# Two self attentions of a decoder: maxima split without a copy, and their fold and row transfers moved inside the round

## The chip, the cores and the metric

The kernel runs on one core of a Trainium2 chip. Its time is the device time of one execution in microseconds, lower is better. The engines are TensorE (PE, its weight loads PEld), VectorE (DVE), ScalarE (ACT), GpSimd (POOL) and SyncE (SP, which only issues transfers). Each engine runs its own instruction stream in order and waits on semaphores.

## The reference

Two decoder layers on x of 8 x 256 x 256 (8 sequences, 256 positions, width 256). Each layer is a self attention, a cross attention and a mixture of experts, each behind a layer norm and added to x. The change touches the two self attentions (16 heads of width 16, causal; the second has 4 groups of keys and values):

```python
scores = jnp.einsum('bhqd,bhkd->bhqk', q, k) / jnp.sqrt(jnp.float32(hd))
scores = scores + (bias + causal)[None]
attn = jax.nn.softmax(scores, axis=-1)
out = jnp.einsum('bhqk,bhkd->bhqd', attn, v)
```

## The kernel before

Each of the five engines has its program written out by hand; `q.wait_ge(at(name, ...))` waits until the event of that name has happened, and `then_inc(*up(name, ...))` signals it. `Banks.take` gives out the eight PSUM banks in rings and makes a taker wait for the last user of the bank.

A self attention (`Attention`, layer L = 0 or 1) works through the 8 batches in rounds i from -2 to 8. Round i attends with batch i and at the same time computes the scores of batch i + 1 for their maxima only. A round has 12 units u, three for each group g of four heads (kind 0, 1 and 2).

- Scores for the maxima (`pe_scores`, lines 462 and 464): twelve groups for each batch; four before the units, the last one, 11, at unit 9. VectorE takes the maxima (`dve_max`, L608).
- `dve_np` (L614 to L620, unit 10) makes minus the maximum into three bf16 parts in `NP`, so that their sum is exact: the first part, the rest `mr` in fp32, the rest rounded to bf16 by a copy, and what is left.
- `pe_fold` (L473) transposes the parts on TensorE. `act_mT` (L716) copies them to SBUF on ScalarE, and `act_mrow` (L737) issues three transfers from ScalarE's queue that put them as rows 101 to 103 into the queries of batch i + 1. All three stood after the 12 units.
- `pe_attend_s` (L482, in each unit) computes transposed scores minus the maxima of batch i. Its first one in a round waits for the three row transfers (event `mrow`). `act_exp` (L721) is the exponential on ScalarE, `pool_keep` (L787) the causal cut on GpSimd.
- `pe_attend_v` (L495 for kinds 0 and 1, L499 for kind 2) multiplies with the values; group g - 1 in units 5, 8 and 11, so group 2 in unit 11. Group 3 comes in the next round, after the first two score groups and before `pe_v` and two more score groups. `act_out` (L727) copies the outputs; `pe_fin1` (L508) and what follows finish the batch.
- Beside this, `act_hi`, `dve_res`, `act_mid`, `pool_lo` (L793) split the queries and keys of batch i + 3 into parts, and `sp_stack` on SyncE stacks them through DRAM into `q_parts` and `k_parts`. `beside` runs one step of other work (layer 0: products for the cross attention, L228 with ctxT; layer 1: its keys and values, lines 1578 to 1676).

Of the kernel before, what the change touches and what calls it, by code (L numbers as in the profile page):

```python
# [10 lines left out]
ALU = mybir.AluOpType  # L11
# [133 lines left out]
def decoder(nc, I, out):  # L145
    with ExitStack() as ctx:
# [144 lines left out]
        def ln_turn(q, s, p, ring):  # L291
            if s not in (2, 5):
                ln_before[s, p] = ln_before.get("now")
                ln_before["now"] = (s, p)
            b, free = banks.take(ring, ("ln", s, p), [("xnT", s, p)])
            q.wait_ge(at("consts", "all"), *free)
            for j in (0, 1):
                q.wait_ge(at("xn", s, 2 * p + j))
                for k in (0, 1):
                    mm = q.e.transpose(PS[b][:, 256 * k + 128 * j:256 * k + 128 * j + 128],  # L300
                                       normed(s, 2 * p + j)[:, 128 * k:128 * k + 128], idf[:, :])
            mm.then_inc(*up("ln_t", s, p))
# [42 lines left out]
        def steps(g, n=1):  # L345

            while n and g:
                if next(g[0], "end") == "end":
                    g.pop(0)
                n -= 1  # L350
# [8 lines left out]
        class Attention:  # L359
# [163 lines left out]
            def tensor(self, q):  # L523
                L, rp = self.L, self.rp
                kv = [kv_tensor(q, rp) if L == 1 else mix_tensor(q, rp)]
                ln_turn(q, self.ln, 0, rp)
                for i in range(-2, B + 1):
                    n, b, f, p = 0 <= i + 1 < B, 0 <= i < B, i >= 1, self.ahead(i)
                    if i < 0:
                        self.pe_qk(q, i + 2, 0)  # L530
                        self.pe_qk(q, i + 2, 1)
                        if i == -2 or L == 1:
                            ln_turn(q, self.ln, i + 3, rp)
                    if n:
                        self.pe_scores(q, i + 1, 0)
                        self.pe_scores(q, i + 1, 1)
                    if f:
                        self.pe_attend_v(q, i - 1, 3)
                    if n:
                        self.pe_v(q, i + 1, 0)  # L540
                        self.pe_scores(q, i + 1, 2)
                        self.pe_v(q, i + 1, 1)
                        self.pe_scores(q, i + 1, 3)
                    for u in range(12):
                        if b:
                            self.pe_attend_s(q, i, u // 3, u % 3)
                        if n and u in self.FIRST:
                            self.pe_scores(q, i + 1, self.FIRST[u])
                        if u == 0 and self.norms(i - 1):
                            ln_turn(q, *self.norms(i - 1), rp)  # L550
                        if L == 0 and u == 2 and i == -1:
                            ln_turn(q, self.ln, 2, rp)
                        if f and u in (1, 2):
                            self.pe_fin1(q, i - 1, u - 1)
                        if p and u in (3, 6):
                            self.pe_qk(q, p, u // 6)
                        if f and L == 0 and u in (7, 8):
                            self.pe_fin2(q, i - 1, u - 7)
                        if b and u in (5, 8, 11):
                            self.pe_attend_v(q, i, u // 3 - 1)  # L560
                        if f and L == 0 and u in (9, 10):
                            self.pe_fin3(q, i - 1, u - 9)
                        self.beside(u, i, kv)
                    if n:
                        self.pe_fold(q, i + 1)
                steps(kv, 999)


# [41 lines left out]
            def dve_np(self, q, b):  # L610

                L, e, m, mr, NP = self.L, q.e, self.m, self.mr, self.NP
                q.wait_ge(at("mx", L, b, 11), at("fold", L, b - 1))
                e.tensor_scalar(NP[:, :, 0, :], m, -1.0, None, ALU.mult).then_inc(*q.step())  # L614
                q.wait_ge(q.chain())
                e.scalar_tensor_tensor(out=mr, in0=m, scalar=-1.0, in1=NP[:, :, 0, :], op0=ALU.mult, op1=ALU.subtract).then_inc(*q.step())
                q.wait_ge(q.chain())
                e.tensor_copy(NP[:, :, 1, :], mr).then_inc(*q.step())
                q.wait_ge(q.chain())
                e.tensor_tensor(NP[:, :, 2, :], mr, NP[:, :, 1, :], ALU.subtract).then_inc(*up("NP", L, b))  # L620

# [122 lines left out]
            def scalar(self, q):  # L744
                L = self.L
                kv = [kv_scalar(q) if L == 1 else mix_scalar(q)]
                self.act_rows(q, 0)
                ln_copy(q, self.ln, 0)
                for i in range(-2, B + 1):
                    n, b, f, p = 0 <= i + 1 < B, 0 <= i < B, i >= 1, self.ahead(i)  # L750
                    if i < 0:
                        self.act_hi(q, i + 2, 0)
                        self.act_hi(q, i + 2, 1)
                        self.act_mid(q, i + 2, 0)
                        self.act_mid(q, i + 2, 1)
                        if i == -2 or L == 1:
                            ln_copy(q, self.ln, i + 3)
                    if f:
                        self.act_out(q, i - 1, 3)
                    for u in range(12):  # L760
                        if u == 1 and self.norms(i - 1):
                            ln_copy(q, *self.norms(i - 1))
                        if L == 0 and u == 3 and i == -1:
                            ln_copy(q, self.ln, 2)
                        if p and u in (4, 7):
                            self.act_hi(q, p, u // 7)
                        if b:
                            self.act_exp(q, i, u // 3, u % 3)
                        if f and L == 0 and u in (8, 9):
                            self.act_fin2(q, i - 1, u - 8)  # L770
                        if p and u in (6, 9):
                            self.act_mid(q, p, u // 9)
                        if b and u == 9:
                            self.act_out(q, i, 1)
                        self.beside(u, i, kv)
                    if n:
                        self.act_mT(q, i + 1)
                        self.act_mrow(q, i + 1)
                steps(kv, 999)


# [786 lines left out]
        def kv_tensor(q, ring):  # L1568
            for c in range(4):
                bk, free = banks.take(ring, ("kv", c), [("kv_f", c)])  # L1570
                q.wait_ge(at("w_cr1", "bp"), at("w_xa", "r"), *free)
                pair_mms(q, PS[bk][:, :], [(ctxT[:, k, 128 * c:128 * c + 128], wkv[:, k, :]) for k in range(2)]).then_inc(*up("kv", c))
                yield
                yield
                bk, free = banks.take(ring, ("kv_v", c), [("kv_vT", c)])
                q.wait_ge(at("kv_f", c), *free)
                for m in range(2):
                    mm = q.e.transpose(PS[bk][:, 128 * m:128 * m + 128], kv_f[:, 256 + 128 * m:384 + 128 * m], idf[:, :])
                mm.then_inc(*up("kv_v", c))
                for _ in range(12):  # L1580
                    yield
                bk, free = banks.take(ring, ("kv_k", c), [("kv_kM", c, 1)])
                q.wait_ge(at("kv_3", c), *free)
                for g in range(8):
                    mm = q.e.transpose(PB[bk][:, 128 * g:128 * g + 128], K3[:, 2 * g:2 * g + 2, :].rearrange("p h c -> p (h c)"), idb[:, :])
                mm.then_inc(*up("kv_k", c))
                yield
            for _ in range(6):
                yield
            bk, free = banks.take(ring, ("kv_q",), [("kv_Vq",)])  # L1590
            q.wait_ge(at("kv_q8"), *free)
            for c in range(4):

                keys = vq[:, :, 256 * (c // 2):256 * (c // 2) + 256].rearrange("p m (n o) -> p m o n", o=2)
                for m in range(2):
                    mm = q.e.transpose(PB[bk][:, 256 * c + 128 * m:256 * c + 128 * m + 128], keys[:, m, c % 2, :], idb[:, :])
            mm.then_inc(*up("kv_q"))
# [582 lines left out]
```

## Time and profile before

| | |
|---|---|
| median of 3 runs | 1379.77 us (1377.14 to 1382.55) |
| the profiled execution | 1379.55 us, its span 1377.5 us |
| TensorE matmuls busy | 1154.4 us, 84% of the span |
| VectorE busy | 897.2 us, 65% |
| ScalarE busy | 632.4 us, 46% |
| GpSimd busy | 577.2 us, 42% |
| mean granted clock of TensorE | 0.913 |

The layer-0 attention runs from the start to about 220 us, the layer-1 attention from about 590 to 790 us. Busy time counts the instructions of an engine, not the issue of transfers. The granted clock is the share of TensorE's 2.4 GHz that it was given.

### The profile page before, as it was taken

The numbers are of one execution on the slowest core, as the hardware profiler recorded it, in microseconds if no ns is written. First come the engines' busy times: TensorE is split into PE (matmuls) and PEld (weight loads), VectorE is DVE, ScalarE is ACT, GpSimd is POOL, SyncE is SP. The second block draws the span as 40 slices with busy tenths as digits, with TensorE's granted clock in tenths as the row PEclk, the third lists the DMA queues.
The fourth block names the chain that finished last, engine by engine and source line by source line (L and its number), as shares of the span: only waits on it lengthen the run. The fifth ranks groups of instructions, "written<-read, shape, count | busy, mean of one in ns | idle before, by whom it ended". The sixth has DMA issues, their size and how long they took to land.

```text
span 1377.5 us, 24811 instructions
## 1 busy us (share of the span) xinstructions
PE 1154.4 (84%) x7679; PEld 811.0 (59%) x7679; DVE 897.2 (65%) x2501; ACT 632.4 (46%) x1432; POOL 577.2 (42%) x886
## 2 busy tenths in 40 slices
PE   3699989983899999767888587778778778999988
PEld 3577757772466666545666345555556555788855
DVE  4576763665333322277977489999999974656557
ACT  3164653331211111214554389888889861433300
POOL 6143542245511111114655444466655654455510
PEclk8799999996899999969998889988888889999999
DMA  5776644112111111155551110000000004455465
GB/s 135 198 209 158 190 109 160 41 47 93 53 46 47 47 47 47 51 164 152 131 147 42 55 75 1 2 33 33 21 21 25 33 32 142 119 159 158 148 179 144
DMA packets 75805, 127.10 MB, mean 92 GB/s; under 512 B 11703, under 2 KB 59063, under 8 KB 72279
## 3 DMA queue, kind: packets, MB, share of 16 engines
q1 hardware_dynamic: 62142, 95.13, 25.1%
q0 software_dynamic: 10272, 28.39, 5.6%
q10 hardware_dynamic: 3264, 2.01, 0.5%
q8 instruction: 65, 1.06, 0.3%
q14 instruction: 62, 0.51, 0.1%
HBM read 76.97 MB, written 48.13 MB: 91 GB/s over the span
## 4 chain that ended last, share of the span: by engine, by line
PE 53%; issue 13%; POOL 11%; ACT 8%; DVE 7%; DMA 5%; SPq 1%; ACTq 1%; POOLq 0%; DVEq 0%
PE ps L228 15%; PE ps L1174 15%; PE ps L1191 7%; ACT work L1911 5%; POOL work L1945 4%; POOL xs_scratch L1505 3%; PE ps L482 3%; DMA W<-work 2%; PE ps L1159 2%; PE ps L1183 2%; PE ps L495 1%; PE ps L464 1%; DVE work L608 1%; PE ps L300 1%; POOL rstd L273 1%
## 5 line engine op out<-in xcount | busy, mean ns | idle before, releaser
L1174 PE MATMUL ps<-W,work 128*128 x628 | 227.9, 496 | 1.5 <-issue 1.4
L1911 ACT ACTIVATE work<-ps,work 128x512 f32<-128x512 f32 x256 | 205.3, 822 | 41.6 <-POOL work L1945 40.5
L1523 POOL DMA_INDIRECT ys_scratch<-work x118 | 113.1, 958 | 262.3 <-DVE work L1367 117.7
L1849 DVE TENSOR_REDUCE work<-ps 128x1 f32<-128x512 f32 x256 | 172.5, 680 | 15.6 <-PE ps L1756 14.9
L1417 DVE TENSOR_TENSOR work<-work,ps 128x128 f32<-128x128 f32 (+1 forms) x118 | 49.7, 421 | 200.9 <-ACT work L1486 200.4
L608 DVE TENSOR_REDUCE work<-ps 128x2 f32<-128x512 f32 (+1 forms) x192 | 127.4, 685 | 72.3 <-PE ps L464 71.0
L787 POOL TENSOR_SCALAR_AFFINE_SELECT work<-work 128x256 f32<-128x256 f32 (+1 forms) x192 | 92.6, 485 | 158.9 <-ACT work L721 157.1
L1945 POOL TENSOR_SCALAR work<-work 128x1 f32<-128x1 f32 x256 | 100.1, 391 | 128.6 <-DVE work L1849 116.0
L1174 PEld LDWEIGHTS ps<-W,work 128*128 128x128 f32 x628 | 110.9, 191 | 69.1 <-issue 62.7
L721 ACT ACTIVATE work<-ps 128x512 f32<-128x512 f32 x192 | 110.3, 598 | 68.2 <-PE ps L482 67.7
L1756 PE MATMUL ps<-SM,work 128*128 128x512 bf16 x256 | 107.1, 420 | 38.3 <-ACT work L1911 33.5
L1486 ACT ACTIVATE work<-ps 128x128 f32<-128x128 f32 (+1 forms) x118 | 45.3, 384 | 165.1 <-PE ps L1174 165.0
L1191 PE MATMUL ps<-W,work 128*128 x470 | 121.0, 380 | 0.0
L1762 PE MATMUL ps<-idf,work 128*128 128x128 f32 x512 | 87.6, 298 | 15.8 <-ACT work L1916 14.3
L1854 DVE TENSOR_SCALAR work<-work 128x1024 bf16<-128x1024 f32 x128 | 93.5, 730 | 3.9 <-ACT work L1911 3.3
L482 PE MATMUL ps<-W 104*128 104x256 bf16 (+1 forms) x512 | 76.2, 258 | 21.9 <-DMA W<-work 14.3
L1191 PEld LDWEIGHTS ps<-W,work 128*128 128x128 f32 x470 | 80.2, 190 | 12.1 <-issue 0.4
L1762 PEld LDWEIGHTS ps<-idf,work 128*128 128x128 f32 x512 | 64.3, 155 | 38.2 <-issue 22.7
L1482 ACT COPY work<-ps 128x256 f32<-128x256 f32 x118 | 44.1, 374 | 85.2 <-PE ps L1159 85.2
L1916 ACT COPY work<-ps 128x512 f32<-128x512 f32 x128 | 80.0, 625 | 5.0 <-PE ps L1762 4.9
L464 PE MATMUL ps<-W 126*128 126x128 bf16 x512 | 71.5, 238 | 12.7 <-DMA W<-q_parts 12.6
L1505 POOL DMA_INDIRECT xs_scratch<-W,work x64 | 71.3, 1114 | 20.4 <-issue 15.7
(261 smaller groups left out, 2367.2 us busy)
## 6 DMA issues: line engine op xcount, KB each, us to landing
work<-xs_scratch SPq DMA_DIRECT2D x79, 132.0 KB, 2.2
W<-ys_scratch SPq DMA_DIRECT2D x16, 512.0 KB, 3.9
q_parts<-work SPq DMA_DIRECT2D x48, 128.0 KB, 2.0
W<-in_w_in SPq DMA_DIRECT2D x6, 1024.0 KB, 11.4
W<-q_parts SPq DMA_DIRECT2D x15, 384.0 KB
work<-xs_scratch SPq DMA_DIRECT2D x39, 130.0 KB, 2.1
W<-k_parts SPq DMA_DIRECT2D x8, 512.0 KB
W<-in_w_out SPq DMA_DIRECT2D x1, 4096.0 KB, 18.9
```

What stands on the lines that cost most here:

```text
L228: mm = q.e.matmul(out_, l, r, start=start and i == 0, stop=i == n - 1, skip_group_check=True)
L482: mm = q.e.matmul(PS[bk][:, w * i:w * i + w], ks[0:NM, h // self.per, 128 * kt:128 * kt + 128], qs[0:NM, h, 256 - w:256], start=i == 0, st ...
L608: q.e.tensor_reduce(self.m[:, j, h0:h0 + n], ov, AX, ALU.max).then_inc(*up("mx", L, b, u))
L721: q.e.activation(self.pt(b, g, kind), PS[banks.of["ps2", L, b, g, kind]][:, :], ACT.Exp, scale=0.25).then_inc(*up("exp", L, b, g, kind))
L1174: mm = q.e.matmul(PS[bks[c]][:, 0:N], self.XT[s % 2][:, k, :], w[:, k, bass.ds(regs[s] + 512 * c if c else regs[s], N)], start=k == 0, sto ...
L1191: mm = q.e.matmul(PS[bk][:, 0:256], self.UT[s % 2][:, 128 * c:128 * c + 128], w[:, bass.ds(regs[s] + 256 * c if c else regs[s], 256)], sta ...
L1505: q.e.indirect_dma_start(XS[L], bass.IndirectOffsetOnAxis(ap=self.idx[:, t, j:j + 1], axis=0), xall[L][:, t, :], None).then_inc(*landing(" ...
L1523: q.e.indirect_dma_start(YS[L], bass.IndirectOffsetOnAxis(ap=self.dst[n % self.NY], axis=0), self.YB[n % self.NY], None).then_inc(*landing ...
L1762: mm = q.e.transpose(PS[bk][:, 128 * c:128 * c + 128], self.eiw[n % 2][:, 128 * c:128 * c + 128], idf[:, :])
L1849: q.e.tensor_reduce(self.mm[:, h:h + 1], PS[banks.of["c1_s", t, h]][:, :], AX, ALU.max, negate=True).then_inc(*up("c1_mx", t, h))
L1911: q.e.activation(self.ee[n // 2 % 3][:, 512 * (h % 2):512 * (h % 2) + 512], PS[banks.of["c1_s", t, h]][:, :], ACT.Exp, bias=self.nb[:, h:h ...
L1945: q.e.tensor_scalar(self.nb[:, h:h + 1], self.mm[:, h:h + 1], self.sq[t % 2][:, h:h + 1], LN255, ALU.mult, ALU.add).then_inc(*up("c1_nb", ...
```

## The change

The copy in `dve_np` goes: the rest is computed twice by the same instruction, once into the bf16 part and once into `mr`, and the two don't wait for one another. The fold moves to unit 11, between the last attend scores and group 2's attend-values. The copy L716 and the three transfers move to unit 11 too, ahead of the round's last exponential (group 3, kind 2).

```diff
@@ TensorE, unit loop @@
                         if f and L == 0 and u in (7, 8):
                             self.pe_fin2(q, i - 1, u - 7)
+                        if n and u == 11:
+                            self.pe_fold(q, i + 1)
                         if b and u in (5, 8, 11):
                             self.pe_attend_v(q, i, u // 3 - 1)
                         if f and L == 0 and u in (9, 10):
                             self.pe_fin3(q, i - 1, u - 9)
                         self.beside(u, i, kv)
-                    if n:
-                        self.pe_fold(q, i + 1)
                 steps(kv, 999)
@@ dve_np @@
                 e.tensor_scalar(NP[:, :, 0, :], m, -1.0, None, ALU.mult).then_inc(*q.step())
                 q.wait_ge(q.chain())
-                e.scalar_tensor_tensor(out=mr, in0=m, scalar=-1.0, in1=NP[:, :, 0, :], op0=ALU.mult, op1=ALU.subtract).then_inc(*q.step())
-                q.wait_ge(q.chain())
-                e.tensor_copy(NP[:, :, 1, :], mr).then_inc(*q.step())
+                for rest in (NP[:, :, 1, :], mr):
+                    e.scalar_tensor_tensor(out=rest, in0=m, scalar=-1.0, in1=NP[:, :, 0, :], op0=ALU.mult, op1=ALU.subtract).then_inc(*q.step())
                 q.wait_ge(q.chain())
                 e.tensor_tensor(NP[:, :, 2, :], mr, NP[:, :, 1, :], ALU.subtract).then_inc(*up("NP", L, b))
@@ ScalarE, unit loop @@
                         if p and u in (4, 7):
                             self.act_hi(q, p, u // 7)
+                        if n and u == 11:
+                            self.act_mT(q, i + 1)
+                            self.act_mrow(q, i + 1)
                         if b:
                             self.act_exp(q, i, u // 3, u % 3)
...
                         self.beside(u, i, kv)
-                    if n:
-                        self.act_mT(q, i + 1)
-                        self.act_mrow(q, i + 1)
                 steps(kv, 999)
```

## Rows read from the trace of the kernel before

**Rows 1.** The list of waits (whole run): total us, times, longest us.

```profile
PE ps L482 <- DMA W<-work: 14.3, 10, 2.8
```

**Rows 2.** The view of line 737: issue ns min/median/max, and the landing.

```profile
L737 ACTq DMA_DIRECT2D W<-work x48: 509/608/1636, 59.5 to 769.1; - x48
...
DMA to landing us min/median/max: 1.8/1.9/5.1
```

**Rows 3.** Timeline of the boundary at 102 us: start us, duration us, engine, line.

```profile
101.38 0.39 PE L482 MATMUL ps<-W 104*128 104x128 bf16 x4
...
101.80 0.60 ACT L721 ACTIVATE work<-ps 128x512 f32<-128x512 f32 x1 [0.23 <-PE ps L482]
...
102.47 0.63 POOL L787 TENSOR_SCALAR_AFFINE_SELECT work<-work 128x512 f32<-128x512 f32 x1 [0.42 <-ACT work L721]
...
102.48 0.28 PE L473 MATMUL ps<-idb,work 128*128 128x128 bf16 x2
...
102.81 0.37 ACT L716 COPY work<-ps 48x256 bf16<-48x256 bf16 x1 [0.41 <-PE ps L473]
...
103.20 1.81 ACTq L737 DMA_DIRECT2D W<-work  x3
...
103.60 0.40 PE L499 MATMUL ps<-work 128*32 128x128 f32 x8
...
106.49 0.39 PE L482 MATMUL ps<-W 104*128 104x256 bf16 x2
```

**Rows 4.** Timeline of the boundary at 705 us.

```profile
704.59 1.09 DVE L618 CAST work<-work 128x32 bf16<-128x32 f32 x1
...
705.72 0.19 DVE L620 TENSOR_TENSOR work<-work 128x32 bf16<-128x32 f32 x1
...
709.34 0.43 PE L499 MATMUL ps<-work 128*32 128x128 f32 x8 [0.55 <-POOL work L787]
...
711.09 0.38 PE L482 MATMUL ps<-W 104*128 104x256 bf16 x2
```

**Rows 5.** Timeline of the boundary at 80 us.

```profile
78.87 0.56 DVE L620 TENSOR_TENSOR work<-work 128x32 bf16<-128x32 f32 x1
...
81.34 0.40 PE L499 MATMUL ps<-work 128*32 128x128 f32 x8
...
84.45 0.39 PE L482 MATMUL ps<-W 104*128 104x256 bf16 x2 [0.28 <-DMA W<-work]
```

**Rows 6.** Timeline of the boundary at 665 us.

```profile
664.91 0.44 DVE L620 TENSOR_TENSOR work<-work 128x32 bf16<-128x32 f32 x1
...
665.74 0.36 ACT L716 COPY work<-ps 48x256 bf16<-48x256 bf16 x1
...
666.53 0.40 PE L499 MATMUL ps<-work 128*32 128x128 f32 x8
...
669.27 0.39 PE L482 MATMUL ps<-W 104*128 104x256 bf16 x2 [0.85 <-DMA W<-work]
```

**Rows 7.** Timeline of the boundary at 128 us.

```profile
126.21 1.99 PE L228 MATMUL ps<-SM,ctxT 128*128 128x256 f32 x8
...
128.72 0.36 ACT L716 COPY work<-ps 48x256 bf16<-48x256 bf16 x1
...
129.15 0.40 PE L499 MATMUL ps<-work 128*32 128x128 f32 x8
...
133.01 0.39 PE L482 MATMUL ps<-W 104*128 104x256 bf16 x2 [1.03 <-DMA W<-work]
```

**Rows 8.** Timeline of the boundary at 202 us.

```profile
202.73 0.42 PE L499 MATMUL ps<-work 128*32 128x128 f32 x8
...
205.91 0.39 PE L482 MATMUL ps<-W 104*128 104x256 bf16 x2 [2.75 <-DMA W<-work]
```

**Rows 9.** Timeline of TensorE, the first attend scores at 189 us.

```profile
189.09 0.39 PE L482 MATMUL ps<-W 104*128 104x256 bf16 x2 [2.40 <-DMA W<-work]
```

**Rows 10.** Stretches: us, busy of PE, PEld, DVE, ACT, POOL, granted clock, DMA share, GB/s.

```profile
190.50:193.90 3.40, 3.40 (x24) 3.11 (x23) 2.01 (x5) 1.45 (x4) 1.13 (x3) 0.54 0.03 5
```

## Prediction

> **What bounds the kernel now.** I read the list of waits, the issue times of the three row transfers and then the timeline at every round boundary of both self attentions (14 boundaries at which one batch's last exponential meets the next batch's maxima, and one before each layer's first batch). The list of waits [rows 1] shows the wait that the change touches: TensorE's first attend scores of a round (L482) stand 14.3 us in ten places until the rows of maxima (the transfers W<-work) have landed. The transfers themselves [rows 2]: each holds ScalarE's queue about 0.6 us while it is issued, and lands about 1.9 us later.
>
> The boundary at 102 us [rows 3] is the pattern. TensorE issues the last attend scores (101.38), attend-values of group 2, the fold (102.48), the next batch's scores, then attend-values of group 3, whose second half (L499, 103.60) needs the last exponential (L721, 101.80) and its causal cut on GpSimd (L787, 102.47). ScalarE does that exponential first, then the copy (102.81), then three issues (103.20 to 105.01). The first attend scores of the new round start at 106.49. The third issue starts about 104.4 and lands 1.9 to 2.0 later [rows 2], at 106.3 to 106.4, and the timeline marks no wait ahead of 106.49: here TensorE had other work almost until the landing, and I take 0.2 us as its wait. TensorE is nearly full in layer 0's rounds, so what it gains or loses at a boundary moves the end.
>
> **The change part by part.**
>
> *Split.* Four chained vector instructions become four with two waits between them. Undisturbed, a link is 0.19 us of work (705.72) and 0.04 of gap before it (704.59 + 1.09 to 705.72) [rows 4]; the new second subtraction waits for nothing and I let half of its link be hidden, so about 0.1 us is saved. The CAST that goes took 1.09 there, longer than its size explains; what comes in its place may be held in the same way. I take 0.1 to 0.35 per boundary, with 0 as the lower bound and 0.9 (1.09 less 0.19) as the upper at three boundaries (645, 685, 705). The Trainium skill, "SBUF — State Buffer", section "Who interferes with whom", says that a VectorE instruction with two SBUF inputs is blocked by a GpSimd instruction that reads SBUF; by it the new second scalar_tensor_tensor would be held as the CAST was and the 0.9 bound would fall to 0; no row here shows it for this instruction.
>
> *Fold ahead of group 2's attend-values.* TensorE does the same work in another order; nothing is gained unless the fold had stood behind other work. When the maxima's parts are late the wait now stands in front of group 2's attend-values, which used to fill it. That hits five boundaries. At 80 us the parts end at 79.43 (78.87 + 0.56) and TensorE, done with that round's attend scores at about 77 (an estimate from the blocks of group 2 and of other work, 1.6 us and more, that then lay before the fold), would stand until then [rows 5].
>
> *Copy and three issues ahead of the last exponential.* This is the large term. ScalarE works in order. From the copy's start to the end of the issues is 2.20 us (102.81 to 105.01), 0.04 to the next instruction, exponential 0.60, 0.07 to GpSimd, cut 0.63, 0.05 to TensorE [rows 3]: the second half of group 3's attend-values can't start before copy + 3.6 us. Before, the exponential was done by the time of the copy. That instruction is in front of the next batch's values and two score groups on TensorE, and those are in front of the first attend scores. The landing itself needs copy + 3.5 (665.74 to 669.27 [rows 6]), so the late exponential, not the landing, sets the boundary nearly always. Group 3's output copy (L727) and the cut's follower on GpSimd (pool_lo, L793, then the SyncE stack for three batches on) wait too; that stack has a round or more of slack except at 182 us.
>
> The boundaries, new start of the first attend scores against old:
> - 102 us: fold after the last attend scores, 101.38 + 0.23 = 101.61, copy 0.33 later (102.48 to 102.81) 101.94, L499 at 105.54 instead of 103.60: +1.94, less the 0.2 of landing wait: +1.75. Two more like it (147, 166 us): +1.9 and, with some 0.4 of landing wait given back, +1.5.
> - 128 us: eight matmuls of other work (L228, 126.21, 1.99 us) stood between [rows 7]. Copy at about 125.66 instead of 128.72, L499 possible at 129.26 against 129.15: +0.1, and the landing wait of 1.03 goes: -0.9.
> - 202 us, last of the layer, no scores in between [rows 8]: the fold can follow the last attend scores some 0.9 sooner, copy 201.5, L499 at 205.1 instead of 202.73, then 0.4 of work: 205.5 against 205.91: -0.4. Its twin in layer 1 (767 us), where the parts are late: 0.
> - 665 us: the parts end at 665.35 (664.91 + 0.44), 0.35 earlier with the shorter chain; copy 665.38, L499 at 668.98 instead of 666.53, remaining work 669.27 - 0.85 - 666.53 = 1.89: 670.87 against 669.27: +1.6 [rows 6]. Its twin at 726 us had a slow landing, which I let absorb most: +0.3.
> - 705 us: parts end 705.91, saved 0.1 to 0.2; copy 706.1, L499 at 709.7 instead of 709.34 (it waited for GpSimd already [rows 4]), then 1.75 of work as before: +0.4. Twin at 645: +0.4.
> - 80 us: parts about 79.1, copy 79.5, L499 at 83.1 against 81.34, less 0.28 of landing wait: +1.5 [rows 5].
> - 182 us: the landing was the latest of all, 2.40 us of waiting before 189.09 [rows 9]. The copy is 0.9 earlier; the traffic that slowed the landing may hold it at the same time: -0.7 (0 to -0.9).
> - 685 and 745 us: group 2 and 3 wait for GpSimd's other work anyway: +0.1 and -0.2. Before the first batches: -0.1 each.
>
> Sum: 1.75 + 1.9 + 1.5 - 0.9 - 0.4 + 0 + 1.6 + 0.3 + 0.4 + 0.4 + 1.5 - 0.7 - 0.1 - 0.2 = **+7.0 us**; with the bounds of the terms +3 to +10.
>
> *Clock.* Ahead of 189.09 TensorE stood 2.40 us [rows 9], and from 190.5 to 193.9 its granted clock was 0.54 with the engine busy all 3.40 us [rows 10]: that is the 1.2 GHz level, worth about 1.7 us. Not every wait need do that. The new stands are 1.9 us at three boundaries, and two near one another at 80, 645, 665, 705 and 726 us (about 1 to 2.2 for the fold, 0.4 to 1.8 for L499). Between none and six such drops, 0 to +10 us; I take two, +3.
>
> **Total.** The profiled execution took 1379.55 us with a span of 1377.5; the median of the three runs is 1379.77, 0.2 above. 1379.55 + 7.0 + 3 = 1389.6; I say **1389.5 us**. A change of 0.5% is 6.9 us, about what a measurement here can tell from none.
>
> **Rivals.**
> 1. *Absorbed, no measurable change* (1381 to 1386). The gains are larger than I give and the later rounds take up the shifts: in layer 1 other waits follow each boundary. For it: half of my sum comes from four boundaries. Against: layer 0's rounds have almost no idle TensorE to absorb with. The +3 end of the sum without a drop of the clock gives 1382.5. 0.27.
> 2. *Issues cost ScalarE little here* and the exponential is late only by the copy. Then L499 is never late: 128, 182, 202 and 767 us gain 0.9, 0.9, 0.9 and 0.5; 102, 166, 665 and 726 us gain 0.2 to 0.4 each; 80 us still loses 1.1 to the fold; sum -3.7: 1376. The Trainium skill, "DMA: Bandwidth & Descriptors", section "Issuing engines are not separate DMA queues", calls the time to initiate a DMA usually small relative to the DMA; the trace disagrees here, 0.6 us each three times over against a landing of 1.9 [rows 2]. 0.05.
> 3. *Faster*: the rows land before TensorE asks for them everywhere and no other wait takes their place, the full 14.3 us of [rows 1]: 1365. It decides where the last cut is done before TensorE reaches L499; that would need 1.9 us more of TensorE work between them at the 102 us boundary, and only 128 us has it. 0.05.
> 4. *Clock*: each fold wait and late exponential drops the clock, six or more times, in layers 0 and 1: 1379.6 + 7 + 10 = 1397 and up. 0.13.
>
> **How the numbers follow.** The forecast (delay of about 7 with zero to three drops, 1386 to 1395) has 0.50. Slower by over 0.5% (above 1386.7): nearly all of it, and rival 4: 0.61. Within 0.5%: rival 1, rival 2 and the forecast's low edge: 0.31. Faster: rival 3 and a little: 0.08. Range for 8 in 10: 1378 to 1398.
>
> **What would show it.** In the profile of the changed kernel the last exponential of a round starts about 2.2 us after the copy L716 begins; L499 waits for POOL L787 at twelve or so boundaries, up to 2 us each, some 15 us in all against almost none in layer 0 now; waits of L482 for W<-work shrink from 14.3 to a few us; the chain that ended last holds ScalarE's issues, L721 and L787 in place of the landing; at 80 us the fold waits 2 us. It is wrong if L499 doesn't wait, if the issues take less, or if the rounds after a boundary make up the time.

## The result, and the profile after

The changed kernel takes 1393.24 us (median of four runs, 1389.79 to 1394.77) against 1378.45 for the kernel before in the same comparison: ratio 1.0118, 95% interval 1.0083 to 1.0153. It is slower, by more than the noise. The profiled execution took 1394.17 us with a span of 1392.1.

The list of waits of the changed kernel (total us, times, longest us), which answers to [rows 1] (code below the split is one line higher now: L715 is the copy, L720 the exponential, L736 the transfers, L786 the causal cut):

```profile
ACT work L720 <- issue: 29.3, 14, 2.8
...
PEld ps L499 <- POOL work L786: 28.1, 16, 2.9
...
PE ps L499 <- POOL work L786: 19.2, 13, 2.4
...
PE ps L473 <- DVE work L619: 17.5, 10, 3.2
...
PE ps L482 <- DMA W<-work: 1.8, 1, 1.8
```

Four lines tell the case. The landing wait that the change touches fell from 14.3 us to 1.8, and what is left stands before layer 0's first batch. In its place TensorE waits 19.2 us in 13 places for the cut (3.0 us before), 17.9 us of it at ten of the boundaries, behind the last exponential, and 17.5 us for the maxima's parts (8.0 before). The first line is the origin of the 19.2: at each of the 14 boundaries the exponential stood behind the issues. In the median those were not dearer than before, as the view of their line shows beside [rows 2]; at five boundaries the three took 2.2 to 2.8 us together in place of 1.8:

```profile
L736 ACTq DMA_DIRECT2D W<-work x48: 510/607/1570, 59.1 to 780.2; - x48
...
DMA to landing us min/median/max: 1.8/1.9/5.3
```

The boundary of [rows 3] is now at 106 us; timeline of the changed kernel:

```profile
105.69 0.39 PE L482 MATMUL ps<-W 104*128 104x128 bf16 x4
...
105.91 0.28 PE L473 MATMUL ps<-idb,work 128*128 128x128 bf16 x2
...
106.23 0.36 ACT L715 COPY work<-ps 48x256 bf16<-48x256 bf16 x1 [0.34 <-PE ps L473]
...
106.62 2.35 ACTq L736 DMA_DIRECT2D W<-work  x3
...
109.02 0.60 ACT L720 ACTIVATE work<-ps 128x512 f32<-128x512 f32 x1 [2.43 <-issue]
...
109.69 0.63 POOL L786 TENSOR_SCALAR_AFFINE_SELECT work<-work 128x512 f32<-128x512 f32 x1 [3.32 <-ACT work L720]
...
110.37 0.43 PE L499 MATMUL ps<-work 128*32 128x128 f32 x8 [2.27 <-POOL work L786]
...
112.19 2.02 PE L228 MATMUL ps<-SM,xnT 128*128 128x256 f32 x4
...
114.43 0.63 PE L482 MATMUL ps<-W 104*128 104x256 bf16 x2
```

Copy, issues, exponential, cut, L499 stand one behind the other, and L499 starts 4.14 us after the copy's start. Then look at L228: four matmuls take 2.02 us where the same four took 1.08 before. The stretches of the changed kernel show why (columns as in [rows 10]): within 2 us of the wait the clock is at its 1.2 GHz level for 3.4 us, with TensorE busy all the time. The other rows are the same behind the boundaries at 80 and 174 us.

```profile
112.00:115.40 3.40, 3.40 (x20) 2.73 (x19) 1.84 (x3) 0.30 (x1) 0.00 (x0) 0.55 0.31 96
...
81.30:84.70 3.40, 3.40 (x20) 2.50 (x13) 0.00 (x0) 0.60 (x1) 1.06 (x2) 0.56 0.04 10
180.30:183.70 3.40, 3.40 (x20) 2.76 (x19) 1.59 (x3) 0.14 (x1) 0.00 (x0) 0.56 0.27 92
```

At the boundary of [rows 5] the loss is of the other kind, a wait for the maxima's parts ahead of group 2's attend-values; L499 comes without a wait but late, since the eight matmuls of other work (L228) ran at the low clock, 3.18 us:

```profile
80.42 0.29 PE L473 MATMUL ps<-idb,work 128*128 128x128 bf16 x2 [2.15 <-DVE work L619]
...
81.87 3.18 PE L228 MATMUL ps<-SM 128*128 128x256 f32 x8
...
85.89 0.40 PE L499 MATMUL ps<-work 128*32 128x128 f32 x8
...
88.56 0.39 PE L482 MATMUL ps<-W 104*128 104x256 bf16 x2
```

From the starts of each batch's first attend scores, layer 0 lost 9.5 us from its first to its last batch (65.76 to 215.44, before 65.74 to 205.91 [rows 8]) and layer 1 5.3 us (635.02 to 782.83, before 628.58 to 771.06): 14.8 us in the rounds. The spans of the two profiled executions differ by 14.6 us, but not by the rounds alone: 3.1 us of layer 0's loss were made up before layer 1's first attend scores, and 2.8 us more were lost behind its last ones, where the two programs are the same. Why is not shown.

### The profile page after: what moved, and what is told of

It is laid out like the page before. It is cut to its first block, busy times and chain, and to the rows that moved or that the text cites. A ratio compares the mean times of both kernels' runs of the same rounds, so it can differ in the third digit from the quotient of the medians.

```text
span 1392.1 us, 24810 instructions
## 1 busy us (share of the span) xinstructions
PE 1160.2 (83%) x7679; PEld 813.4 (58%) x7679; DVE 895.3 (64%) x2501; ACT 633.4 (46%) x1432; POOL 578.9 (42%) x886
## 4 chain that ended last, share of the span: by engine, by line
PE 53%; issue 13%; POOL 10%; ACT 9%; DVE 8%; DMA 3%; SPq 1%; ACTq 1%; another core or an unknown queue 0%; POOLq 0%; DVEq 0%
PE ps L228 16%; PE ps L1173 15%; PE ps L1190 7%; ACT work L1910 5%; POOL work L1944 4%; POOL xs_scratch L1504 3%; PE ps L482 2%; PE ps L1158 2%; PE ps L1182 2%; DVE work L608 2%; PE ps L464 1%; ACTq L736 1%; PE ps L300 1%; ACT work L720 1%; DMA W<-q_parts 1%
## 5 line engine op out<-in xcount | busy, mean ns | idle before, releaser
L786 POOL TENSOR_SCALAR_AFFINE_SELECT work<-work 128x256 f32<-128x256 f32 (+1 forms) x192 | 92.5, 484 | 172.5 <-ACT work L720 171.3
L720 ACT ACTIVATE work<-ps 128x512 f32<-128x512 f32 x192 | 111.0, 599 | 96.6 <-PE ps L482 67.0
L1173 PEld LDWEIGHTS ps<-W,work 128*128 128x128 f32 x628 | 110.9, 191 | 69.0 <-issue 62.6
L1761 PEld LDWEIGHTS ps<-idf,work 128*128 128x128 f32 x512 | 65.6, 157 | 38.6 <-issue 23.6
L482 PE MATMUL ps<-W 104*128 104x256 bf16 (+1 forms) x512 | 75.7, 256 | 9.4 <-ACT work L720 7.4
```

The lines of the kernel that those rows point to most:

```text
L720: q.e.activation(self.pt(b, g, kind), PS[banks.of["ps2", L, b, g, kind]][:, :], ACT.Exp, scale=0.25).then_inc(*up("exp", L, b, g, kind))
L1173: mm = q.e.matmul(PS[bks[c]][:, 0:N], self.XT[s % 2][:, k, :], w[:, k, bass.ds(regs[s] + 512 * c if c else regs[s], N)], start=k == 0, sto ...
L1761: mm = q.e.transpose(PS[bk][:, 128 * c:128 * c + 128], self.eiw[n % 2][:, 128 * c:128 * c + 128], idf[:, :])
```

## The experiments

All ratios are against the kernel before on the same chip, with 95% intervals.

**The split alone** (the hunk of `dve_np`, nothing else).

> Only the split of the maxima changes. Theory A (the last exponential stands behind the copy and three issues on ScalarE): about 1 to 2 us less than before over 16 batches, ratio 0.998 to 1.001. Rival F (the fold's wait on TensorE in front of group 2's attend-values is the cost): the same. A rival that the split itself costs (held by GpSimd): ratio 1.003 or more.

Measured 1.0023 [0.9997, 1.0050]. No gain that can be told, and no loss. The profile says where the hoped-for part went. At 715 us in the changed kernel (the boundary of [rows 4]) the long CAST is gone and the two subtractions take 0.62 together, but the last step is now held:

```profile
714.33 0.18 DVE L614 TENSOR_SCALAR work<-work 128x32 bf16<-128x32 f32 x1
...
714.55 0.62 DVE L617 SCALAR_TENSOR_TENSOR work<-work 128x32 bf16<-128x32 f32 x2
...
714.99 1.19 POOL L792 TENSOR_TENSOR work<-aux,work 128x512 bf16<-128x512 f32 x1
...
715.20 1.03 DVE L619 TENSOR_TENSOR work<-work 128x32 bf16<-128x32 f32 x1
```

It ends, at 716.23, just after GpSimd's L792 at 716.18. Before, it was the CAST that ended, at 705.68 [rows 4], just after GpSimd's same instruction:

```profile
704.49 1.16 POOL L793 TENSOR_TENSOR work<-aux,work 128x512 bf16<-128x512 f32 x1
```

So the hold passed from the CAST to the last step.

**The fold alone** (TensorE's two hunks).

> Only the fold moves ahead of group 2's attend-values; split, copy and transfers as before. Theory A: the fold's waits for the maxima's parts grow from 8 to some 17 us, but group 3's second half (L499) is not late; ratio 1.000 to 1.004. Rival F: most of the loss of the whole change, ratio 1.008 to 1.012.

Measured 1.0155 [1.0124, 1.0186]: above both theories, mine by most. The timeline shows one boundary with most of the loss. The first attend scores behind it come 32.25 us after those of the first batch (64.04), where they came 18.71 after them before (65.74 to 84.45 [rows 5]): 13.5 us, of 21.4 us that the rounds of both layers lost in this execution:

```profile
78.96 0.40 PE L473 MATMUL ps<-idb,work 128*128 128x128 bf16 x2 [2.51 <-DVE work L620]
...
80.73 3.78 PE L228 MATMUL ps<-SM 128*128 128x256 f32 x8
...
84.55 0.58 ACT L935 COPY SM<-ps 128x512 f32<-128x512 f32 x1 [6.52 <-PE ps L228]
...
85.03 0.36 ACT L716 COPY work<-ps 48x256 bf16<-48x256 bf16 x1
...
85.42 1.79 ACTq L737 DMA_DIRECT2D W<-work  x3
...
96.29 0.61 PE L482 MATMUL ps<-W 104*128 104x256 bf16 x2 [7.78 <-DMA W<-work]
```

The fold's wait delays the other work's matmuls; the copy of their product (L935) is ahead of the maxima's copy on ScalarE; so the rows go out at 85.4 instead of about 81.3, and land 9.3 us after their issue (median) instead of 1.9. In the stretch from 86 to 97 us the DMA engines are 95% busy with the next batch's stack and the expert weights.

**The copy and the issues alone** (ScalarE's two hunks).

> Only the copy and the three issues move ahead of the last exponential; the fold stays at the end of the round, so the copy is as late as before and the exponential later than with the whole change. Theory A: L499 comes copy + 3.6 us at all 14 boundaries, about 2.8 us later than before at those of layer 0; ratio 1.018 to 1.030, slower than the whole change. Rival F: no fold wait is added; ratio 0.998 to 1.003.

Measured 1.0221 [1.0189, 1.0254], as theory A has it. In its list of waits L499 waits 35.6 us for the cut, against 19.2 in the changed kernel: the copy is later by the fold's place, and the exponential with it. The rounds lose 31.1 us.

**The issues behind the exponential.**

```diff
                         if n and u == 11:
                             self.act_mT(q, i + 1)
-                            self.act_mrow(q, i + 1)
                         if b:
                             self.act_exp(q, i, u // 3, u % 3)
+                        if n and u == 11:
+                            self.act_mrow(q, i + 1)
```

> The whole change, but the three issues stand behind the last exponential (the copy stays ahead of it). Theory A: the exponential is late only by the copy, the rows land about 0.6 us later than with the whole change; the loss goes, ratio 0.996 to 1.002 against before. Rival F: the fold's wait is as in the whole change; ratio 1.008 to 1.012.

Measured 0.9987 [0.9965, 1.0008]. Fold and copy stay where the change put them, only the issues pass behind the exponential, and the whole loss is gone. What is left of the change is no gain either: the interval reaches over 1. Timeline of the same boundary in this run; L499 is 1.69 us behind the copy, not 4.14:

```profile
107.08 0.37 ACT L715 COPY work<-ps 48x256 bf16<-48x256 bf16 x1 [0.34 <-PE ps L473]
...
107.35 0.59 ACT L720 ACTIVATE work<-ps 128x512 f32<-128x512 f32 x1
...
107.48 1.81 ACTq L736 DMA_DIRECT2D W<-work  x3
...
108.77 0.40 PE L499 MATMUL ps<-work 128*32 128x128 f32 x8
```

**One transfer, and six.** The 48 source rows go into the three destination rows in one transfer, or each of the three is cut into two of eight heads.

```diff
-                for c in range(3):
-                    q.e.dma_start(self.qs[b % 3][101 + c:102 + c, :, :], self.mT[16 * c:16 * c + 16, :])...
+                q.e.dma_start(self.qs[b % 3][101:104, :, :], self.mT[0:48, :])...
```

> The whole change with the three row transfers as one (48 source rows into 3 destination rows). Theory A: one issue instead of three ahead of the last exponential, which comes 1.2 us sooner; at the 14 boundaries L499 is late by 0.7 instead of 1.9 us: some 12 us less than the whole change, ratio 1.001 to 1.006 against before. Rival W (what counts is when the rows land or the fold's wait, not how long ScalarE is held): 1.009 to 1.013.

> The whole change with six row transfers of eight heads each instead of three: 1.8 us more on ScalarE ahead of the last exponential. Theory A: 14 times up to 1.8 us more, ratio 1.024 to 1.034 against before. Rival W: the rows land later too, by 1.8 us, but that wait was nearly gone; ratio 1.012 to 1.018.

Measured 0.9957 [0.9938, 0.9976] and 1.0452 [1.0415, 1.0488]. So the loss turns on how long ScalarE is held ahead of the exponential. The line of the issues, one transfer and then six:

```profile
103.16 0.76 ACTq L735 DMA_DIRECT2D W<-work  x1
```

```profile
112.14 3.93 ACTq L738 DMA_DIRECT2D W<-work  x6
...
116.11 0.60 ACT L720 ACTIVATE work<-ps 128x512 f32<-128x512 f32 x1 [4.00 <-issue]
...
117.46 0.66 PE L499 MATMUL ps<-work 128*32 128x128 f32 x8 [3.85 <-POOL work L788]
```

The exponential starts 0.27, 1.2, 2.24 and 4.37 us after the copy's start with 0, 1, 3 and 6 issues ahead of it (2.24 where the three took their usual 1.8 us; 2.79 at 106 us). Rival W is out. Both went past what I had written (1.001 to 1.006, 1.024 to 1.034): with one transfer the landing, too, is sooner by two issues (L482's waits for it 1.4 us in all), but the rounds of the profiled execution still take 2.8 us more than before's, so why the run is faster than before is not shown; with six the low clock comes on top (mean granted clock 0.892, against 0.909 with the whole change), and two late landings of 10.0 us together.

**The transfers from SyncE.** All three, ahead of the low parts' writes of `sp_stack`, or by themselves where no stack is left to do.

```diff
                         if n and u == 11:
                             self.act_mT(q, i + 1)
-                            self.act_mrow(q, i + 1)
@@ sp_stack @@
                 for c, made in enumerate(("hi", "mid", "lo")):
+                    if c == 2 and b >= 2:
+                        self.act_mrow(q, b - 2)
@@ sync @@
                         self.sp_stack(q, self.ahead(i))
+                    elif 0 <= i < B - 1:
+                        self.act_mrow(q, i + 1)
```

> The whole change, but the three row transfers are issued by SyncE between the writes of the middle and the low parts of the batch three on. Theory A: the exponential is late only by the copy and the rows land as early as with the whole change; ratio 0.993 to 0.999 against before. Rival Q: SyncE's queue is behind with weights and stacks, the rows go out late and L482 waits again for W<-work by 15 us or more: 1.005 or more.

Measured 0.9952 [0.9934, 0.9971], theory A. L499 waits 1.7 us in all and L482 3.1 us for its rows; the rounds are 1.3 us shorter than before.

**The fold behind group 2's attend-values.**

```diff
-                        if n and u == 11:
-                            self.pe_fold(q, i + 1)
                         if b and u in (5, 8, 11):
                             self.pe_attend_v(q, i, u // 3 - 1)
+                        if n and u == 11:
+                            self.pe_fold(q, i + 1)
```

> The whole change, but the fold stands behind group 2's attend-values (still ahead of the work beside). Theory A: where the parts are ready the copy and with it L499 come about 0.8 us later than with the whole change, where they are late group 2's values fill the wait; both of some 6 us, ratio 1.009 to 1.015. Rival F (the fold's wait is the larger cost, by the drops of the clock that follow it): 1.003 to 1.007.

Measured 1.0167 [1.0138, 1.0197]: above what I wrote for either theory, and by 0.5% above the whole change, though the two intervals overlap. With the issues ahead of the exponential every delay of the copy is a delay of L499, and L499's wait for the cut grows from 19.2 to 29.3 us, while the fold's falls from 17.5 to 8.2. So with the issues where the change has them, the fold's early place did no harm; that it helped is within the noise.

**Fold moved, copy and issues directly behind the exponential.** To settle the run with the fold alone: the same, but copy and issues ahead of the other work (the diff is against that run).

```diff
                             self.act_exp(q, i, u // 3, u % 3)
+                        if n and u == 11:
+                            self.act_mT(q, i + 1)
+                            self.act_mrow(q, i + 1)
...
                         self.beside(u, i, kv)
-                    if n:
-                        self.act_mT(q, i + 1)
-                        self.act_mrow(q, i + 1)
```

> As the run with the fold alone moved (which lost 1.55%), but copy and three issues stand directly behind the last exponential, ahead of the round's last work beside. Theory C (the fold alone lost because its copy still stood behind the work beside, whose matmuls the fold's wait had delayed, so that the rows went out into the stack and weight traffic): ratio 0.997 to 1.003 against before. Rival F (the fold's wait itself and the clock after it): 1.010 or more.

Measured 1.0017 [0.9997, 1.0037], theory C; rival F, with the cost in the fold's wait itself, is out. The fold's wait is as long as there (2.51 us), the rows go out 5 us earlier and nothing waits for them at this boundary:

```profile
79.72 0.29 PE L473 MATMUL ps<-idb,work 128*128 128x128 bf16 x2 [2.51 <-DVE work L620]
...
80.04 0.36 ACT L716 COPY work<-ps 48x256 bf16<-48x256 bf16 x1 [1.26 <-PE ps L473]
...
80.43 1.79 ACTq L737 DMA_DIRECT2D W<-work  x3
...
86.22 0.38 PE L482 MATMUL ps<-W 104*128 104x256 bf16 x2
```

**Better versions.** The first is the whole change with the two edits above together (one transfer, from SyncE). The second keeps the split of before, has the fold behind group 2's attend-values and the copy directly behind the last exponential, and the same one transfer from SyncE; its edits are pieces of the diffs above.

> The whole change with one row transfer, issued by SyncE. With theory A nothing of the exponential's delay is left to gain against three transfers from SyncE (0.9952), only the landing comes 1.2 us sooner, where L482 waited 3.1 us in all: ratio 0.992 to 0.997 against before.

> The split of before; fold behind group 2's attend-values, copy behind the last exponential, both ahead of the work beside; one row transfer issued by SyncE. Nothing on TensorE or ScalarE is then held that was not before, and the rows land 1.2 us sooner than before and more where work beside stood ahead: L482's waits for W<-work under 3 us, the fold's 8 us as before; ratio 0.989 to 0.995 against before. If the fold's wait in front of group 2 costs nothing after all, as e11_sync_one.

The whole change with one transfer issued by SyncE takes 1362.87 us against 1377.92: 0.9900 [0.9871, 0.9928], a little past what I wrote, and the fastest kernel of this study. The other order takes 1368.37, 0.9950 [0.9927, 0.9973], at the edge of what I wrote. The spans of the two profiled executions are equal (1362.4 and 1362.3), but the second's is among the fastest of its twelve runs (1362.61 to 1375.78), while all six of the first lie between 1360.63 and 1364.76. So the whole change's order is the faster one here; the two differ in the split, the fold's place and the copy's, and which of them counts was not tried. The list of waits of the first:

```profile
PE ps L473 <- DVE work L619: 17.7, 10, 3.2
...
PE ps L482 <- DMA W<-work: 1.7, 2, 1.2
...
PE ps L499 <- POOL work L784: 1.2, 4, 0.4
```

The fold still waits as in the changed kernel, the other two waits are nearly gone.

One comparison over all these runs: how much longer than before the rounds of both layers took in the profiled execution, against the difference of the medians. For the losses the two agree: 14.8 us in the rounds and 14.8 by the medians (whole change), 21.4 and 21.9 (fold alone), 31.1 and 29.9 (copy and issues alone), 24.2 and 23.6 (fold behind the values), 59.1 and 62.6 (six transfers). For the gains they don't: 2.8 us longer in the rounds but 4.8 us faster (one transfer), 1.3 and 5.7 us faster (from SyncE), 3.5 and 15.1 (both together), 4.5 and 9.6 (the other order). So where the losses arise is shown. That the better versions are faster is shown too, but the traces place only a part of it in the rounds.

## Why the prediction was right, point by point

- *Copy and three issues ahead of the last exponential: copy + 3.6 us to L499.* Right in mechanism and size. L499 came 3.59 us after the copy at 7 of 14 boundaries, all with issues of the usual 1.8 us (in five of them with a wait marked before it), and up to 4.6 where they took up to 2.8. The last exponential came 2.24 us after the copy, where 2.2 was forecast; L499's waits at the boundaries were 17.9 us in ten places, where about 15 in twelve were. Shown by moving the issues behind the exponential (1.0118 to 0.9987) and by one and six transfers.
- *The boundaries.* +1.75 at 102 us was +3.8: the three issues took 2.35 us, L499's wait was 2.27 instead of 1.9, and the clock took the rest. Two of the kind gave +2.1 and +3.5 (1.9 and 1.5 predicted), 128 us -0.8 (-0.9), 182 us -1.2 (-0.7), 202 us -1.9 (-0.4; the round before it no longer has the low clock of [rows 10]), 645 us +0.6 (+0.4), 665 us +2.3 (+1.6), 685 us +1.2 (+0.1), 705 us +2.9 (+0.4), 726 us +0.8 (+0.3), 745 us -1.7 (-0.2), 767 us -0.7 (0). The signs held at all where I gave one of over 0.1; the sum, 7.0 without the clock, was 14.8 with it. The single boundaries missed by 12 us upward and 4 us downward together, so that the sum is no further off owes something to luck.
- *80 us: +1.5 by the fold's wait.* Too small: +4.1. The wait (2.15 us) is as told, but the boundary was not set by the late exponential: copy + 3.6 would have let L499 start at 84.3, and it started at 85.89 because TensorE was behind. 1.2 us of that are the low clock over the matmuls behind it, and another 1.3 us came from a stretch at the low clock in the round before (granted clock 0.56 from 67.7 to 71.1), of which I can't show that the change caused it. This one doesn't need the issues: with them behind the exponential it lost as much, 4.0 us.
- *Clock: two drops, +3.* The term was mis-sized, and with it the total: 10 us were forecast and 14.8 measured. In layer 0's rounds there were four such stretches of 3.4 us after the change (from 67.7, 81.3, 112.0 and 180.3 us) where there had been one (190.5), three of them right behind a new wait. At up to 1.7 us each, as from [rows 10], the three more explain some 4 to 5 us (an estimate) of the 7.8 us between sum and measurement. For the rest I have the longer issues (0.4 to 1.0 us over the forecast's 1.8 at 5 boundaries, 3.2 in all) and layer 1, where low stretches came and went in both kernels and I can't divide them.
- *The split.* 0.1 to 0.35 us a boundary; nothing measurable came of it, and the 0.9 bound for the long CAST did fall to about 0.2: from the first to the last step 1.90 us at 715 us, 2.08 before. What was held was not the second subtraction, which I had named as the candidate, but the last step, 1.03 us and to within 0.05 us of the end of GpSimd's L792. The Trainium skill, "SBUF — State Buffer", section "Who interferes with whom", says that a VectorE instruction with two SBUF inputs contends with a GpSimd instruction that reads SBUF; the last step has two, and the trace agrees.
- *Rivals 1 and 4*, a shift absorbed by the later rounds and six or more drops of the clock: the measured time lies between theirs. Layer 0's rounds kept a loss of 9.5 us, and they had four low stretches.
- *Rival 2, issues that cost ScalarE little* is out by the series of 0, 1, 3 and 6 issues: 0.7 to 0.9 us each. The Trainium skill, "DMA: Bandwidth & Descriptors", section "Issuing engines are not separate DMA queues", calls the time to initiate a DMA usually small relative to the DMA. That does not fit these transfers of 8 KB: 0.6 us each to issue, against 1.9 us from issue to landing.
- *Rival 3, faster*: what I called its condition, 1.9 us more work between, can also be met from the other side, by taking the issues off ScalarE. With one transfer from SyncE that gave 15 us by the medians. That this is about the 14.3 us of [rows 1] is luck: L482's waits for the rows fell by 12.6 us, but the fold's rose by 9.7. Of the 15.0 us between the two spans 3.5 are in the rounds and 2.7 ahead of layer 0's first attend scores; 2.8 lie between the two layers' rounds and 6.0 behind the last ones, where the program is as before. The same last stretch was shorter than in the kept trace of before, by 2.3 to 6.4 us, in ten of the eleven runs above, the slower ones among them, so that part is not the better version's doing as far as these traces tell.

## What to carry to other kernels

A transfer issued from ScalarE held ScalarE here for 0.6 us or more: ask what stands behind it and who waits for that, and count each issue. Moving the transfers ahead came out faster here when they went to SyncE's queue or were made one. Issued by ScalarE, three of them were at their best directly behind the exponential, and that was no faster than before. Before moving a wait forward on the critical engine, look at what used to fill it, and at what a later start will collide with: the same three 8 KB transfers landed in 2 us or in 9.

## What the runs showed of the hardware that I had not expected

Waits of 2.15 and 2.27 us in an otherwise full TensorE (at 80 and 110 us) were followed within 2 us by 3.4 us at the 1.2 GHz level (granted clock 0.56 and 0.55), so such a wait cost up to 1.7 us beyond its length; the one of 2.40 us ahead of 215.08 was not, nor was one of 2.51 us in the run with copy and issues directly behind the exponential (granted clock 1.00 from 79.7 to 83.1), while in the run with the fold behind the values the last wait before such a stretch (80.8 to 84.2, granted clock 0.50) was of 0.65 us, so the length of one wait does not tell whether the clock falls. And 48 partitions of 512 bytes went into three partitions as one transfer with one issue of 0.73 us (median; 0.76 at 103 us), in place of three of 0.6 each.
